# A graph network in four layers on one core: another order for the work beside TensorE in the third layer

## What is computed

```python
def _L2_gnn_ref(states, adj, W_msg, b_msg, W_ih, W_hh, b_ih, b_hh):
    agg = adj @ states
    msg = relu(agg @ W_msg.T + b_msg)
    gi, gh = msg @ W_ih.T + b_ih, states @ W_hh.T + b_hh      # split in three: r, z, n
    r, z = sigmoid(i_r + h_r), sigmoid(i_z + h_z)
    n = tanh(i_n + r * h_n)
    return (1.0 - z) * n + z * states

def _L3_gnn_ref(x, adj, embed, layer, embed_bias, layer_bias):
    h = h_mul(x, embed)                     # exp_map_zero(log_map_zero(x) @ W)
    h = h_add(h, embed_bias[None, :])       # a sum on the hyperbolic ball
    neigh = exp_map_zero(adj @ log_map_zero(h))
    out = h_mul(concatenate((x, neigh), axis=1), layer)
    return h_add(out, layer_bias[None, :])

h = maximum(layernorm(x), 0); x = x + _L0_gnn_ref(h, adj, ...)   # attention
h = maximum(layernorm(x), 0); x = x + _L1_gnn_ref(h, adj, ...)   # mean of the neighbours
h = maximum(layernorm(x), 0); x = x + _L2_gnn_ref(h, adj, ...)   # gated unit
h = maximum(layernorm(x), 0); x = x + _L3_gnn_ref(h, adj, ...)   # hyperbolic
```

## Time and profile before

| what | value |
|---|---|
| time, median of 3 runs | 628.37 us (626.72 to 628.53) |
| the profiled execution's own time | 626.34 us |
| its span, first to last instruction | 624.5 us |
| TensorE busy | 571.3 us, 91% |
| VectorE, ScalarE, GpSimd busy | 338.7, 217.7, 99.8 us |
| mean granted TensorE clock | 0.984 |

### The profile page before, as it was taken

One profiled execution on the slowest core, in us unless ns is written; L12 is line 12 of the kernel. 1 busy time (PEld: TensorE's weight loads), 2 busy tenths in 40 slices (PEclk: granted clock), 3 DMA queues, 4 the chain that ended last, 5 costly groups with the idle time before them and its releaser, 6 DMA issues.

```text
span 624.5 us, 12573 instructions
## 1 busy us (share of the span) xinstructions
PE 571.3 (91%) x4599; PEld 354.9 (57%) x4599; DVE 338.7 (54%) x1483; ACT 217.7 (35%) x588; POOL 99.8 (16%) x104
## 2 busy tenths in 40 slices
PE   5589999999899899999999998998999899999981
PEld 5489899999754455554444453443544444554541
DVE  5872553221333433333434866866866844577786
ACT  5430000000001111111125586686686573523433
POOL 4860100000000000000001121111111110321311
PEclk9879999999999999999999999999999999999996
DMA  8999999999900000000000000000000011101000
GB/s 230 108 108 108 108 109 109 108 108 109 96 2 2 1 1 1 0 1 1 1 0 1 18 18 2 17 18 1 17 9 10 17 38 48 34 35 52 17 35 34
DMA packets 13650, 27.01 MB, mean 43 GB/s; under 512 B 1056, under 2 KB 1696, under 8 KB 13600
## 3 DMA queue, kind: packets, MB, share of 16 engines
q0 software_dynamic: 8704, 16.78, 26.7%
q1 hardware_dynamic: 4896, 9.51, 4.4%
HBM read 72.43 MB, written 4.19 MB: 123 GB/s over the span
## 4 chain that ended last, share of the span: by engine, by line
PE 60%; DVE 17%; ACT 12%; issue 6%; POOL 2%; DVEq 1%; DMA 1%; another core or an unknown queue 1%; SPq 0%; ACTq 0%; POOLq 0%
PE acc L1432 35%; PE acc L1252 9%; PE acc L1253 9%; ACT w L1072 4%; PE acc L1279 3%; POOL region_st L941 2%; ACT region_st L1148 1%; DVE region_st L754 1%; ACT L1078 1%; DVE region_st L751 1%; ACT L1083 1%; DVE region_st L369 1%; PE acc L1286 1%; PE acc L1272 1%; POOL rs L941 1%
## 5 line engine op out<-in xcount | busy, mean ns | idle before, releaser
L1432 PE MATMUL acc<-adj,hs_a 128*128 128x512 fp8e4 x1024 | 230.2, 379 | 2.0 <-DVE hs_a L526 1.0
L1432 PEld LDWEIGHTS acc<-adj,hs_a 128*128 128x128 f16 x1024 | 98.6, 98 | 112.8 <-issue 1.7
L1252 PE MATMUL acc<-region_op,adj 128*128 128x133 f16 x1024 | 127.1, 224 | 8.5 <-issue 3.6
L1253 PE MATMUL acc<-region_op,adj 128*128 128x132 f16 x1024 | 127.1, 223 | 0.0
L1432 PE MATMUL acc<-adj,region_op 128*128 128x512 fp8e4 x512 | 119.6, 379 | 0.0
L1252 PEld LDWEIGHTS acc<-region_op,adj 128*128 128x128 fp8e4 x1024 | 101.1, 99 | 11.1 <-DMA adj<-adj_pieces 4.4
L1253 PEld LDWEIGHTS acc<-region_op,adj 128*128 128x128 fp8e4 x1024 | 101.1, 99 | 0.1
L1432 PEld LDWEIGHTS acc<-adj,region_op 128*128 128x128 f16 x512 | 49.0, 98 | 54.8 <-issue 4.0
L941 POOL TENSOR_TENSOR region_st<-region_st,small 128x4 f32<-128x4 f32 (+1 forms) x39 | 45.1, 1157 | 212.7 <-ACT w L1072 140.0
L941 POOL TENSOR_TENSOR rs<-rs,small 128x4 f32 (+3 forms) x27 | 30.4, 1129 | 286.5 <-DVE rs L363 268.4
L1054 ACT ACTIVATE hs_a<-rowbuf 128x512 f32 x8 | 5.0, 629 | 137.9 <-DVE rowbuf L369 137.9
(11 more groups left out here) (238 smaller groups left out, 691.7 us busy)
## 6 DMA issues: line engine op xcount, KB each, us to landing
adj<-adj_pieces POOLq DMA_DIRECT2D x32, 512.0 KB, 66.1
p_rows<-rowbuf SPq DMA_DIRECT2D x8, 256.0 KB, 2.0
region_op<-p_rows SPq DMA_DIRECT2D x8, 256.0 KB, 3.1
out_rows<-x SPq DMA_DIRECT2D x7, 256.0 KB, 2.0
x<-x_rows SPq DMA_DIRECT2D x3, 512.0 KB, 6.7
region_st<-matrices SPq DMA_DIRECT2D x1, 768.0 KB, 8.9
x<-x_rows SPq DMA_DIRECT2D x2, 256.0 KB, 3.9
out_rows<-x SPq DMA_DIRECT2D x2, 128.0 KB, 1.7
```

The lines of the kernel that those rows point to most:

```text
L1252: mm(bank[TG + it % TG][:, 0:HI], adj8[:, it, jt, :], op0[:, jt, 0:HI], start=(jt == 0), stop=False)
L1253: last = mm(bank[TG + it % TG][:, 0:LO], adj8[:, it, jt, :], op0[:, jt, HI:OPW], start=False, stop=(jt == NT - 1))
L1432: last = mm(dst, hs[:, jt, part, :], adj8[:, c * TG:(c + 1) * TG, jt, :], start=(k == 0), stop=(k == 2 * NT - 1))
```

## The change

The loops of VectorE and ScalarE become eleven written-out steps i = 0 to 10 over four groups: i (`now`), i - 1 (`before`), i - 2 (`second`), i - 3 (`third`). `layer2` falls into small functions with the same instructions. On ScalarE a step begins with the copy `h3T16` of group i - 2 and the logarithms; the copy `hT` comes before the copy of the aggregate and waits for VectorE's `hidden_sum` (a new semaphore, `sum_ready`) where it waited for the whole update. On VectorE the tanh's argument comes first, the dots with the bias and the point on the ball of group i - 2 stand ahead of the new gate, and the tangent rows are those of group i - 3. GpSimd's loop takes `norm_z` of a group one place later. On TensorE `message` stands at k = 9 and `hidden_gates` at 10; the own transposes at 43; `own_part` at 43 and ahead of `embed` at 48; `update_back` at 53.

```diff
@@ GpSimd
             inverse_deviation(0, 2 * NG)
-            with pool.Fori(1, NG) as g:
+            norm_h(0)
+            norm_e(0, 0)
+            inverse_deviation(1, 2 * NG)
+            with pool.Fori(2, NG) as g:
                 norm_h(g - 1)
+                norm_z(g - 2)
                 norm_e(g - 1, 0)
                 inverse_deviation(g, 2 * NG)
-                norm_z(g - 1)
             norm_h(NG - 1)
+            norm_z(NG - 2)
             norm_e(NG - 1, 0)
             norm_z(NG - 1)
@@ VectorE, in place of layer2(a, b, c) and its loop
+            def hidden_sum(g):
+                dve.wait_ge(S["pre_hT"], g + NG + 1)
+                if g:
+                    dve.wait_ge(S["ssh_ready"], g)
+                v.tensor_tensor(dT, hT16[:, 0, :], hT16[:, 1, :], ALU.add).then_inc(S["sum_ready"], 1)
...
+            for i in range(NG + 3):
+                now, before, second, third = i < NG, 0 <= i - 1 < NG, 0 <= i - 2 < NG, 0 <= i - 3 < NG
+                if second:
+                    tanh_argument(i - 2)
+                if now:
+                    low_aggregate(i, NG)
+                if third:
+                    low_tangent(i - 3)
+                if before:
+                    new_rows(i - 1)
+                if second:
+                    bias_dots(i - 2)
+                if before:
+                    low_rows(i - 1)
+                if second:
+                    ball_point(i - 2)
+                if now:
+                    new_gate(i)
+                    hidden_sum(i)
+                if 0 <= i - 1 <= NG:
+                    norms_in(i - 1)
+                if now:
+                    update(i)
+                if 0 <= i - 1 <= NG:
+                    norms_out(i - 1)
+                if now:
+                    residual(i)
@@ ScalarE, in place of layer2(s, b, c) and its loop
+            for i in range(NG + 3):
+                now, before, second, third = i < NG, 0 <= i - 1 < NG, 0 <= i - 2 < NG, 0 <= i - 3 < NG
+                if second:
+                    rows_T(i - 2)
+                if 0 <= i - 2 <= NG:
+                    n = i - 2
+                    logarithms(H_ONLY if n == 0 else Z_ONLY if n == NG else BOTH, n + 1)
+                if now:
+                    if i:
+                        act.wait_ge(S["sum_ready"], i)
+                    own_rows_T(i, NG)
+                if second:
+                    embedded_squares(i - 2)
+                if third:
+                    high_tangent(i - 3)
+                if now:
+                    high_aggregate(i, NG, False)
+                if second:
+                    own_product(i - 2)
+                    tanh_of(i - 1)
+                if now:
+                    messages(i)
+                if before:
+                    high_rows(i - 1)
+                    rows_squares(i - 1)
+                if now:
+                    gates(i)
+                if second:
+                    ball_squares(i - 2)
+                if now:
+                    candidate(i)
@@ TensorE
             def own_part(s):
+                pe.wait_ge(S["h3T_ready"], s - NG + 1)
                 if s > NG:
                     pe.wait_ge(S["p1_ready"], s - NG)
...
-            own = {1: {50: own_transposes, 60: own_self}, 2: {62: own_transposes}, 3: {}}
+            own = {1: {50: own_transposes, 60: own_self}, 2: {43: own_transposes}, 3: {}}
             after = {1: {8: neighbours},
-                     2: {1: hidden_gates, 6: message, 11: message_gates},
+                     2: {9: message, 10: hidden_gates, 11: message_gates},
                      3: {}}
-            late = {15: new_transposes, 26: embed, 32: own_part}
-            back = {44: update_back}
+            late = {15: new_transposes, 43: own_part, 48: embed}
+            back = {53: update_back}
...
-                    if k in late and NG <= s - 2 < 2 * NG - 1:
+                    if k in late and NG <= s - 2 < 2 * NG - 1 and (s < FIRST or k < 36):
                         late[k](s - 2)
...
             aggregate(FIRST, 0, 36)
+            own_part(FIRST - 2)
+            embed(FIRST - 2)
             update_back(FIRST - 1)
...
             new_transposes(FIRST - 1)
+            own_part(FIRST - 1)
             embed(FIRST - 1)
-            own_part(FIRST - 1)
```

More of the change, by code:

```diff
@@ L826, in _, with event, new_rows @@
-            layer2(0, None, None)
-            layer2(1, 0, None)
-            with dve.Fori(2, NG) as g:
-                me.loop(g - 2, STEPS_2)
-                layer2(g, g - 1, g - 2)
-            me.end(NG - 2)
-            layer2(None, NG - 1, NG - 2)
-            layer2(None, None, NG - 1)
+            def event(n):
+                part = H_ONLY if n == 0 else Z_ONLY if n == NG else BOTH
+                return part, n + 1
+            def new_rows(g):
+                dve.wait_ge(S["rs_ready"], g + 2 * NG + 1)
+                normalised(g, lambda t: tile(dT, t)).then_inc(S["xnew_ready"], 1)
@@ new lines, in residual, with low_tangent @@
+            def residual(g):
+                dve.wait_ge(S["uT_full"], g + 1)
+                v.tensor_tensor(x[:, group_of(g), :], x[:, group_of(g), :], tiles(bank[7]), ALU.add).then_inc(S["x3_ready"], 1)
+                dve.wait_ge(S["x3_ready"], g + 1)
+                statistics(g)
+            def low_tangent(g):
+                dve.wait_ge(S["bhi_ready"], g + 1)
+                v.tensor_tensor(hs_a[:, group_of(g), 1, :], tiles(z_rows), hs_a[:, group_of(g), 0, :],
+                                ALU.subtract).then_inc(S["hs_ready"], 1)
+                dve.wait_ge(S["hs_ready"], g + 2 * NG + 1)
@@ new lines, in ball_squares, with high_tangent @@
+            def ball_squares(g):
+                act.wait_ge(S["z_ready"], g + 1)
+                act.wait_ge(S["ssh_ready"], min(g + 2, NG))
+                square_sums(lambda t: tile(z_rows, t), col4(SSZ)).then_inc(S["sqz_ready"], 1)
+            def high_tangent(g):
+                act.wait_ge(S["coef_ready"], g + 1)
+                act.wait_ge(S["sqz_ready"], g + 1)
+                for t in range(TG):
+                    r = tile(z_rows, t)
+                    last = a.activation(r, r, ACT.Copy, scale=col4(COEF)[:, t:t + 1])
+                last.then_inc(S["zs_ready"], 1)
+                act.wait_ge(S["zs_ready"], g + 1)
+                a.activation(hs_a[:, group_of(g), 0, :], tiles(z_rows), ACT.Copy).then_inc(S["bhi_ready"], 1)
```

184 lines of the change are left out of this document (69 added, 115 removed).

## The result

The changed kernel takes **611.56 us** (median of 4 runs, 611.1 to 613.44), the kernel before beside it 628.21 (4 runs). The ratio of the runs is 0.9752, with a 95% interval of 0.9736 to 0.9769, which is 15.6 us gained (14.5 to 16.6); the two medians by themselves are 16.65 apart. The forecast was 614.4, in a range of 611 to 621, so the result lies 0.6 us above the range's lower end. The profiled execution took 611.1 us, 609.3 of them its span, 15.2 less than the span before.

The account below looks back on a forecast made before the run. TensorE, busy 91% of 624.5 us, was taken as the bound, so only its waits count: hT 5.2 + h3T 7.0 + message 2.0 - 0.6 + 0.25 = 13.9 us gained; 628.37 - 13.9 = 614.4 us, range 611 to 621.

Parts of the forecast that it names:

- hT: TensorE's hidden gates wait for ScalarE's copy hT in the third layer; this wait goes, 5.2 us gained.
- h3T: TensorE's embed waits for ScalarE's copy of the new rows; 8.3 us lost, all but 1.3 gained, 7.0.
- message: TensorE's message gates wait for the message in the third layer; this wait goes, 2.0 us gained.
- way back: TensorE's wait for VectorE's update in the last layer's first stage grows from 0.8 to 1.4 us, 0.6 lost.
- tangent: Last aggregates wait for VectorE's last tangent rows, 0.5 us; half counted as gone, 0.25 gained.
- The message gates: Timetable entry for TensorE's six message-gate records in a stage: 2.68 us, ending at 7.65 of a 21.8 us stage.
- The spares: Time between ready and wanted in a stage: message 0.3, message gates 1.1, h3T 1.5, update 2.0 us.
- The last h3T wait: The very last group's copy h3T has nothing to hide it; wait stays, on own_part, 1.2 listed, 1.3 lost.
- (2): One wait a stage stays, eight waits give back 6.5 us: 7.4 gained, 621.0 us; chance 0.14.
- (3): Written-out VectorE and ScalarE code costs more per instruction, making the kernel slower: 643 us; chance 0.05.
- (4): ScalarE's table switches cost more in their new place, 9 us given back: 623.5 us; chance 0.03.
- (5): Waits go, but the last layer's VectorE chain ends the kernel anyway: no change; chance 0.03.

Follow-up runs that it names:

- the message run: Changed kernel with TensorE's message behind 5 aggregates instead of 9, nothing else moved: 616.86 us, ratio 0.9827 to the kernel before.
- the written-out old order: Kernel before with only the third layer's loops of VectorE and ScalarE written out as plain code: 621.49 us, ratio 0.9917 to before.
- own transposes late: Changed kernel with the transposes of the next own rows back behind 62 aggregates instead of 43: 638.7 us, ratio 1.019 to the kernel before.
- embed early: Changed kernel with TensorE's embed back behind 26 aggregates and own_part behind 32, embed first again: 622.64 us, ratio 0.9936 to the kernel before.
- the engines' order alone: Changed kernel's order on VectorE, ScalarE and GpSimd, all TensorE stages at their old places: 675.27 us, ratio 1.0753 to the kernel before.
- the two slow experiments: The runs with own transposes late (638.7 us) and with the engines' order alone (675.27 us).

## Why the prediction was right, step by step

**The sum.** In the two traces the last group's aggregates start 15.24 us earlier; forecast 13.9. By terms, forecast and measured: hT 5.2 and 5.2; h3T 7.0 and 7.1; message 2.0 and 2.0; way back -0.6 and -0.57 (it now loses 1.19 + 0.16 = 1.35, forecast 1.4); tangent 0.25 and 0.48. The measured ones are the waits of the one trace less those of the other. These make 14.2, and 0.2 more was gained ahead of the layer, where nothing changed. Two terms were mis-sized.

- *The message gates.* In all eight stages before, the first fp32 matmul (two records) took 0.49 to 0.53 us from its first record to its second, in the changed kernel 0.43 (L1329 in the earlier trace rows has 1.12 us for the pair, L1401 above 1.02). The 2.68 us for the six records in the timetable, read in a stage that waits, thus held 0.10 of time lost; over the layer it is 3 x 0.057 + 5 x 0.105 = 0.70. Hence a stage of 21.65, not 21.8. That makes 15.1 of 15.24; 0.1 to 0.2 is not placed. That the 0.057 of the three stages without a listed wait is lost time of the same kind, and not another cause, is argued, not shown.
- *The tangent rows.* I counted half of this wait as gone, without a working. All went:

```profile
511.19 0.69 DVE L845 TENSOR_TENSOR hs_a<-region_st,hs_a 128x512 f16<-128x512 f32 x1 [2.01 <-ACT hs_a L1198]
```

The ends of this chain, before and in the change: the last copy h3T, VectorE's first operation on the tanh's result, and, before, the last tangent rows.

```profile
506.02 1.02 ACT L1130 ACTIVATE region_st<-acc 128x1024 f16<-128x1024 f16 x1 [1.28 <-PE acc L1272]
515.03 0.16 DVE L736 TENSOR_TENSOR region_st<-region_st 128x4 f32<-128x4 f32 x1
526.74 0.69 DVE L818 TENSOR_TENSOR hs_a<-region_st,hs_a 128x512 f16<-128x512 f32 x1 [2.01 <-ACT hs_a L1151]
```

```profile
491.27 1.02 ACT L1161 ACTIVATE region_st<-acc 128x1024 f16<-128x1024 f16 x1 [2.29 <-PE acc L1344]
499.48 0.16 DVE L735 TENSOR_TENSOR region_st<-region_st 128x4 f32<-128x4 f32 x1
```

From the end of the last copy h3T (492.29) to the end of these rows is 19.6 us; before it was 20.4 (507.05 to 527.43). The 0.8 goes in the step between. Before, ScalarE did own_product, the table load and the tanh, then the tangent rows' copies of the group ahead; VectorE did the low part of those rows (0.69) behind the copies, and only behind that the ball's scale, which took the tanh's result at 515.03, 7.98 us after h3T. Now the copies come first, their low part lies beside ScalarE's table load, and VectorE takes the tanh's result at 499.48, 7.19 us after h3T. The prediction had this order before it and did not follow it through the last group.

**The time.** The traces differ by 15.24 us, well within the ratio's 14.5 to 16.6; the medians' 16.65 stands at its edge. The forecast set 13.9 against a median that stood 2.0 above its own profiled execution; after the change the median stands 0.5 above. Of the 2.8 us between 614.4 and 611.56, then, 1.3 is the sum, and the rest is how runs scatter about a profiled one.

**The spares.** Message 0.3 forecast, 0.42 measured; message gates 1.1 and 1.40; h3T 1.5 and 1.90; update 2.0 and 2.83. All came out larger, the longest chain's by most. One reason is seen in the rows: the sums add whole durations, while neighbours on an engine start before the one ahead has ended (on ScalarE L1165 starts at 418.45, 0.09 before L1129 ends); that it is the whole reason is not shown. The prediction knew this and used it only for the way back. Its 1.4 there was a middle taken between two bounds and not worked out, so that 1.35 came so near it is partly luck.

**The last h3T wait.** It stays, on own_part, 1.1 listed, near the 1.2 forecast.

**The rivals.** (2), one wait a stage, fell; the message run shows how near it was: 0.42 us. (Its 8 x 0.8 is 6.4, not 6.5, which moves nothing.) (3), dear written-out code, fell: linked operations of VectorE in the changed kernel (count, busy us, mean ns, idle before),

```profile
L705 DVE SCALAR_TENSOR_TENSOR region_st<-region_st 128x8 f32<-128x8 f32 (+1 forms) x28 | 4.6, 166 | 1.0
```

wait 1.0 / 28 = 0.036 us each, the loop's in the earlier trace rows 0.033, and the written-out old order is faster than its loop. (4), dearer table switches, fell: the rows above have 1.28 us for a load, and the operation that needs it starts 0.01 later. The Trainium skill, ScalarE: Activation LUTs, section "What ACT_TABLE_LOAD costs", gives about 2.66 us for a switch with its drain; the trace has 1.31 from the end of the operation ahead (L1183, 417.03) to the start of the one behind (418.34), and the measurement decides. (5) fell: the last layer's aggregates start earlier, and the end came 15.2 us earlier with them.

**What the prediction left out.** That the hidden gates' new place is also needed for the bank that ScalarE reads late, and that the transposes' new place carries ScalarE's whole order. Both were in the change and the forecast held without them, but whoever had kept one of the old places would have lost 10 to 27 us.

## What to carry to other kernels

Where one engine is busy nearly all the time, list for each thing that it waits for when it is ready and when it is wanted, and move wants and ready times together: one half of this change (the engines' order without TensorE's places) made this kernel 7.5% slower, the whole 2.5% faster. Look first at what stands at the head of an in-order queue, for a step that the busy engine can do late at no cost to itself (19 aggregates' delay of a transpose) can hold up all that stands behind its result on another. The timetable that adds whole durations gave spares that were too small in all four places here, so its small positive ones held; but take each duration from a stretch that doesn't wait.

## What the runs showed of the hardware

TensorE's granted clock fell at some of its waits and came back. With the own transposes late, by windows, stages 13 and 14, each from shortly before the end of a wait of 3.22 us (length, PE, PEld, DVE, ACT, POOL, clock, DMA share, GB/s):

```profile
409.00:413.00 4.00, 3.14 (x15) 1.57 (x16) 3.85 (x15) 3.33 (x6) 0.00 (x0) 1.00 0.17 66
434.00:439.00 5.00, 4.09 (x12) 1.54 (x13) 4.70 (x20) 4.03 (x8) 0.00 (x0) 0.66 0.15 54
```

and the nine hidden-gate matmuls behind those waits on TensorE, in the same order:

```profile
410.74 2.11 PE L1358 MATMUL acc<-hT,region_st 128*128 128x512 f16 x9
...
436.22 3.35 PE L1358 MATMUL acc<-hT,region_st 128*128 128x512 f16 x9
```

At the lower level, 1.2 GHz, matmuls started 0.427 us apart instead of 0.216, eight in a row, and the stage took 26.73 instead of 25.05: 1.7 us on top of the wait. In that run six stages wait, 2.28 us in one and 3.22 in five; four of these waits were followed by a fall, the one of 2.28 among them, two were not (the one shown, and the last); after waits of 1.66 us (embed early) the clock stayed at 1.00 and matmuls 0.216 apart. But length alone does not tell: one wait in the second layer (for hT, 1.9 to 2.0 us listed) stands in all ten traces, and in one of them, that of the engines' order alone, the clock fell there too. So a long wait can cost this kernel more than its own length, and that is why the two slow experiments came out above what was expected of them. What decides whether the clock falls at a given wait was not tried.
